# Where tail steps, table turns and weight rounding stand in a recommendation kernel's hand-written order

## The reference

```python
e = jnp.stack([tbl_0[ids[:, 0]], ..., tbl_25[ids[:, 25]]], axis=1)   # 2048 x 26 x 128
combined = jnp.concatenate([e, dense_x[:, None, :]], axis=1)
interact = jnp.einsum('bfd,bgd->bfg', combined, combined)            # 27 x 27 each sample
z = interact[:, _TRIU_I, _TRIU_J]                                    # 351 pairs
h = jnp.concatenate([z, dense_x], axis=1)
h = jnp.maximum(h @ W_top1 + b_top1, 0.0)                            # 479 -> 512
h = jnp.maximum(h @ W_top2 + b_top2, 0.0)                            # 512 -> 256
y = h @ W_top3                                                       # 256 -> 1
```

## Time and profile before

| | us |
|---|---|
| Median of 3 runs | 474.73 (464.82 to 482.69) |
| The profiled execution | 459.81 |
| Its span in the trace | 458.0 |
| PE busy | 431.6 (94%) |
| ACT busy | 282.5 (62%) |
| POOL busy | 253.6 (55%) |
| DVE busy | 241.7 (53%) |

### The profile page before, as it was taken

One profiled execution on the slowest core, in us unless ns is written; L12 is line 12 of the kernel. 1 busy time (PEld: TensorE's weight loads), 2 busy tenths in 40 slices (PEclk: granted clock), 3 DMA queues, 4 the chain that ended last, 5 costly groups with the idle time before them and its releaser, 6 DMA issues.

```text
span 458.0 us, 8937 instructions
## 1 busy us (share of the span) xinstructions
PE 431.6 (94%) x3418; PEld 406.1 (89%) x3418; DVE 241.7 (53%) x279; ACT 282.5 (62%) x996; POOL 253.6 (55%) x270
## 2 busy tenths in 40 slices
PE   4789999789999999999999999999999999979997
PEld 3679999679998999999999999999999898878896
DVE  3979895731667345581567525682467714411152
ACT  3445746857476665667557674666667575677642
POOL 5556565666566656655665656656565556665000
PEclk9999999899999999999999999999999999999999
DMA  6764333121212211221212211221122211111000
GB/s 180 232 210 130 95 91 102 53 65 57 65 47 64 69 53 47 63 70 43 71 50 60 59 54 47 65 68 42 59 59 63 65 54 46 44 45 46 2 1 0
DMA packets 17706, 31.36 MB, mean 68 GB/s; under 512 B 5594, under 2 KB 8480, under 8 KB 17664
## 3 DMA queue, kind: packets, MB, share of 16 engines
q0 software_dynamic: 8384, 17.19, 13.7%
q1 hardware_dynamic: 8400, 12.81, 8.9%
q10 hardware_dynamic: 880, 0.80, 0.6%
HBM read 30.76 MB, written 0.01 MB: 67 GB/s over the span
## 4 chain that ended last, share of the span: by engine, by line
PE 86%; DMA 5%; ACT 4%; issue 3%; DVE 1%; SPq 1%; ACTq 0%
PE x_ps L589 32%; PE gram_ps L603 25%; PE tail_ps L657 13%; PE x_ps L570 6%; DMA hot_in<-in_tbl 5%; PE tail_ps L636 3%; PE tail_ps L627 3%; ACT gram L386 2%; PE tail_ps L663 1%; DVE onehot L841 1%; ACT xt L363 1%; PE x_ps L692 0%; ACT z L400 0%; PE tail_ps L703 0%; PE x_ps L686 0%
## 5 line engine op out<-in xcount | busy, mean ns | idle before, releaser
L553 POOL DMA_INDIRECT raw<-in_tbl,ids_sb x262 | 252.7, 964 | 168.3 <-issue 91.6
L841 DVE TENSOR_TENSOR onehot<-ids_wide,row_ps 128x1024 fp32r<-128x1024 int16 (+1 forms) x175 | 195.0, 1154 | 84.6 <-PE x_ps L589 67.7
L589 PE MATMUL x_ps<-onehot,hot_hi 128*128 128x256 f32 x616 | 159.5, 294 | 9.1 <-DVE onehot L841 3.8
L386 ACT COPY gram<-gram_ps 32x104 f32<-32x104 f32 x496 | 117.9, 238 | 63.6 <-PE gram_ps L603 50.5
L589 PE MATMUL x_ps<-onehot,hot_lo 128*128 128x256 f32 x616 | 151.7, 282 | 0.0
L603 PE MATMUL gram_ps<-xt 128*128 128x108 f32 x1024 | 129.8, 277 | 2.7 <-ACT xt L791 1.0
L589 PEld LDWEIGHTS x_ps<-onehot,hot_hi 128*128 128x128 f32 x616 | 116.1, 189 | 16.4 <-issue 11.8
L603 PEld LDWEIGHTS gram_ps<-xt 128*128 128x128 f32 x1024 | 121.8, 191 | 5.9 <-ACT gram L386 2.0
L589 PEld LDWEIGHTS x_ps<-onehot,hot_lo 128*128 128x128 f32 x616 | 116.1, 189 | 0.0
L363 ACT COPY xt<-x_ps 128x128 f32<-128x128 f32 (+1 forms) x104 | 47.9, 515 | 41.0 <-PE x_ps L589 35.7
L453 DVE TENSOR_TENSOR h_lo<-h,h_hi 128x256 fp32r<-128x256 f32 x28 | 11.9, 426 | 66.6 <-ACT h L425 53.8
(11 more groups left out here) (74 smaller groups left out, 317.8 us busy)
## 6 DMA issues: line engine op xcount, KB each, us to landing
ids_wide<-in_hot_ids SPq DMA_DIRECT2D x19, 256.0 KB
raw<-in_tbl,ids_sb POOLq DMA_INDIRECT x262
hot_in<-in_tbl SPq DMA_DIRECT2D x14, 256.0 KB, 3.3
hot_in<-in_tbl SPq DMA_DIRECT2D x6, 320.0 KB, 3.8
weights_in_place<-in_w SPq DMA_DIRECT2D x6, 128.0 KB
dense_sb<-in_dense_t ACTq DMA_DIRECT2D x6, 128.0 KB
dense_sb<-in_dense_t SPq DMA_DIRECT2D x2, 128.0 KB
w1d_sb<-in_w SPq DMA_DIRECT2D x2, 128.0 KB
```

Of the source, the lines that this page charges most:

```text
L386: last = copy(gram[rows, :, per_fill * i:per_fill * (i + 1)], src)
L553: nc.gpsimd.indirect_dma_start(out=raw[k][:, f, :], out_offset=None, in_=sources[f], in_offset=bass.IndirectOffsetOnAxis(ap=ids_sb[:, t, f ...
L589: last = nc.tensor.matmul(ps, table[:, chunk_at[j] + c, :], moving[:, c - a, :], start=(c == 0 and table is tables_of[0]), stop=(c == chun ...
L841: nc.vector.tensor_tensor(columns(p), ids_wide[:, it // IDS % IDS_RING, it % IDS, 0:width].unsqueeze(1).to_broadcast([P, n, width]), row_n ...
```

## The change

Five edits in the order and around it:

1. A tail step that was due ahead of a tile's second gram of a pair is put behind that gram, so that grams of a block's first tile come in pairs.
2. `with_turn` spreads a tile's turns evenly over a run of slots, and so between the pieces of an item; copies to `xt` then come in another order than the fills of the banks, and the waits count copies (`copied_no`).
3. The casts of the first layer's weights move from block 0's last grams to three items of block 1's lookup ahead of them, their residues to grams 1, 3 and 5 of block 0's second tile; the second layer's two go to the first two grams of block 1. PE asks for each layer's halves where it needs them.
4. The first layer's weights are padded on the host to blocks of 128 rows, with a semaphore a block; what is computed with them is unchanged.
5. DVE makes an item's first piece ahead of the residue of its table, not behind it.

```diff
-    def with_turn(slots, t, ends):
+    def with_turn(slots, t, first, last):
         n = len(turn_groups[t])
         for g in range(n):
-            slots[ends[-(-(g + 1) * len(ends) // n) - 1]].append(("turn", t, g))
+            slots[first + round(g * (last - first) / (n - 1))].append(("turn", t, g))
...
-            slots += with_turn(slots[-1:] + hot[held:lead], t + 1, [0] + ends if h > 0 else ends[-2:])[1:]
+            n = lead - held
+            slots += with_turn(slots[-1:] + hot[held:lead], t + 1, 0 if h > 0 else n - 7, n - 1)[1:]
...
-            slots += with_turn([[] for _ in range(n_gram + n)], t + 2, [n_gram + g for g in range(n)])
+            slots += with_turn([[] for _ in range(n_gram + 3 * n)], t + 2, n_gram, n_gram + 3 * n - 3)
...
-        for i, steps in before.items():
+        moved = {}
+        for i in sorted(before):
+            second = slots[i] and slots[i][0][0] == "gram" and slots[i][0][1] % 2 == 1
+            moved.setdefault(i + 1 if second else i, []).extend(before[i])
+        for i, steps in moved.items():
             slots[i][:0] = steps
...
-        weights_at_gram = range(gram_block + 1 - len(weight_parts), gram_block + 1)
+        second = [("gram", gram_block + n) for n in range(len(weight_parts) - n_kz)]
+        round_at = [("hot", item_start[nh + 2 + n]) for n in range(n_kz)] + second
+        split_at = [("gram", n_gram + 1 + 2 * n) for n in range(n_kz)] + second
...
-                    sp.dma_start(w1z_at[0:kz[k], k, part], w1[sum(kz[:k]):sum(kz[:k + 1]), part]).then_inc(weights_in, 16)
+                    sp.dma_start(w1z_at[:, k, part], w1[k * P:(k + 1) * P, part]).then_inc(weights_in[k], 16)
...
-                    if what[0] in weights_at_gram:
-                        act.wait_ge(weights_in, n_weights * 16)
-                        hi, _, src = weight_parts[weights_at_gram.index(what[0])]
-                        copy(hi, src).then_inc(weights_rounded, 1)
+                if (kind, *what) in round_at:
+                    n = round_at.index((kind, *what))
+                    act.wait_ge(weights_in[n], 2 * 16)
+                    hi, _, src = weight_parts[n]
+                    copy(hi, src).then_inc(weights_rounded, 1)
...
                 if p == item_start[it]:
-                    if it == first_item[j] and j not in direct:
-                        hot_residue(j)
...
                                         ALU.is_equal).then_inc(piece_ready, 1)
+                if p == item_start[it] and it == first_item[j] and j not in direct:
+                    hot_residue(j)
```

More of the change, by code:

```diff
@@ L189, in build @@
                 lead += 1
-            ends = [end + 1 for end in item_ends(hot[held:lead])[:-1]]
-            slots += with_turn(slots[-1:] + hot[held:lead], t + 1, [0] + ends if h > 0 else ends[-2:])[1:]
-        else:
-            slots += gram_slots(t) + with_turn([[] for _ in turn_groups[t + 1]], t + 1, list(range(len(turn_groups[t + 1]))))
+            n = lead - held
+            slots += with_turn(slots[-1:] + hot[held:lead], t + 1, 0 if h > 0 else n - 7, n - 1)[1:]
+        else:
+            n = len(turn_groups[t + 1])
+            slots += gram_slots(t) + with_turn([[] for _ in range(n)], t + 1, 0, n - 1)
             lead, beside = 0, 0
@@ L226, in build @@
     fill_no = {step: n for n, step in enumerate(fills)}
+    copies = [("hot", s[1]) if s[0] == "held" else ("hot", pieces[s[1]][0]) if s[0] == "hot" else s for s in order
+              if s[0] in ("turn", "held")
+              or (s[0] == "hot" and s[1] + 1 in item_end and pieces[s[1]][0] not in held_items)]
+    copied_no = {step: n + 1 for n, step in enumerate(copies)}
+    assert sorted(map(str, fills)) == sorted(map(str, copies))
     def pieces_made():
@@ L896 @@
     rest = len(halves[0]) - 64
[L897 removed]
+    pair_rows = [halves[0][:rest], halves[1][:P], halves[0][rest:] + halves[1][P:]]
     w1 = np.asarray(inputs["W_top1"])
```

45 lines of the change are left out of this document (25 added, 20 removed).

## The result

The change made the kernel slower: 478.5 us (median of four, 473.85 to 481.56) against 469.77 us of the kernel before, ratio 1.027, 95% interval 1.021 to 1.033. Forecast were 469 us, 458 to 478, and no measurable change. The profiled execution of the change took 479.47 us, that of the kernel before 459.81 us.

The account below looks back on a forecast made before the run. PE was taken as the bound, busy 431.6 of 458.0 us. Terms -4.0 - 0.7 - 1.9 - 2.2 + 3.2 = -5.6 us gave 454.2 from 459.81, scaled by 474.73/459.81 to 469 us, range 458 to 478.

Parts of the forecast that it names:

- Turns between pieces: Lookups: turns between an item's pieces give the ring time to fill, taking half of 3.8 us of PE waits, -1.9 us.
- The warning in the last part: Sign of being wrong: casts between items delay `xt` copies so that PE waits between 57 and 66 us.
- Pairs: First tiles: neighbouring `zt` groups and grams run in a row, 0.5 us in each of four settled blocks, -2.2 us in all.
- The new wait of 0.8 us ahead of part 3: Settled blocks: part 3 waits for part 1's bank, its Relu copies queued behind others; 0.8 us four times, +3.2 us.
- Edits 3 and 5: Column stage: moved casts end waits and the half clock, -4.0 us; start: first piece ahead of the residue, -0.7 us.
- Padding: Weight loads: 128-row blocks use more transfer engines, giving gathers up to 3.0 us; 0 in the sum.
- The gathers set the end: Rival, chance 0.20: PE's savings end in a wait for gathers before the last turns; about 473 us.
- The clock falls again: Rival, chance 0.12: idle PE in the column stage drops the clock again, leaving -3.4 us; scaled 471 us.
- Its remark that the one fall before stood behind the emptiest stretch: Support for the clock rival: the trace's one clock fall in 458 us comes behind its emptiest stretch.
- Slower: Rival, chance 0.06: pairs fill both product banks and PE waits for gram copies in first tiles; +12 us, scaled 487.

Follow-up runs that it names:

- e1: The change with turns put back behind whole items, all else kept: 455.79 us, 1.000 of the kernel before.
- e3: The change with both the turns between pieces and the paired grams undone: 454.98 us, 1.002 of the kernel before.
- k3: The change with a column step that would move behind a gram pair put ahead of it: 464.96 us, 1.016 of the kernel before.
- e2: The change with tail steps put back ahead of each gram group, turns still between pieces: 462.99 us, 1.018 of the kernel before.
- d2: The change with ScalarE made late by three small copies ahead of every second hot item's copy: 471.61 us, 1.034 of the kernel before.
- g1: The change with four x_ps banks instead of three, row numbers read from SBUF: 482.79 us, 1.055 of the kernel before.
- e4: The change with turns back behind whole items and tail steps right behind a pair's second gram: 453.78 us, 0.996 of the kernel before.
- k1: e4 with a column step that would stand inside a pair put ahead of it: 453.07 us, 0.992 of the kernel before; again 453.83 us, 1.001.
- d1: The kernel before with ScalarE made late by three small copies ahead of every second hot item's copy: 459.28 us, 1.012 of the kernel before.
- m3: The kernel before with gathers in bursts of four behind the first 66, nothing else changed: 509.09 us, 1.104 of the kernel before.
- g0: The change, unaltered, run again on chip B: 461.25 us, 1.012 of the kernel before.
- g2: The change with block 0's turns alone at their old places: 458.15 us, 1.009 of the kernel before.
- g3: The change with each settled block's last turn ahead of the held item moved behind the split item: 457.0 us, 1.004 of the kernel before.
- m1: k1 with gathers in bursts of four behind the first 66: 506.74 us, 1.100 of the kernel before; on chip A 443.95 us, 0.978.
- k2: k1 with all gathers in bursts of four in place of three: 452.17 us, 0.998 of the kernel before.

## Why the prediction was wrong

**Edit 2, the failed step.** "Turns between pieces: -1.9, bounds 0 and -3.8". The bound at 0 was wrong: I costed what a turn between pieces fills, and not the bank that a split item keeps. With three banks in a ring, the two fills after an item's first piece decide how soon its bank is wanted again, and here they came inside the item. On chips without late engines the term is +5.5 us with edit 1 there (461.25 against 455.79, on two chips; ratios 1.012 and 1.000, whose intervals touch) and +8.0 us without it (462.99 against 454.98, on one chip; 1.018 and 1.002, apart). In three settled blocks it is +2.7 us, of which 1.9 are waits and 0.8 PE's own longer work. My own row showed the danger: 1.2 us of waits for `xt` copies, which I counted as something to win. The warning in the last part, that casts between items might delay `xt` copies, named the right releaser with the wrong cause.

**Pairs.** The gain is there, but smaller: eight zt records in a row take 0.47 us, as in the earlier trace rows, and PE's busy time in three blocks fell from 156.48 (both back) to 155.69 with edit 1, 0.3 us a block against the 0.5 forecast. The new wait of 0.8 us ahead of part 3 came as worked out: 0.8 at its longest, six times, 3.9 us in all when run again (forecast +3.2 in four); up to 1.4 in the first profile with ScalarE late. Edit 1 as a whole is +0.8 us by the medians (e1 against e3, not resolved) and +1.7 in three blocks, against +1.0 in four. What I missed is the last block: a wait of 2.5 us and a half clock of 10.2 us.

**Edits 3 and 5.** The column stage came 3.5 us shorter (forecast -4.0), with casts at 57.9, 59.8 and 63.2 us. The same stage, counted as the same 187 PE records, took 24.1 to 24.8 us in eight other profiles with the casts moved, but 26.3 us in k3, 27.3 in e2 and d2, 30.8 in e1 and 32.1 in g1, in all of which the clock fell again between 88 and 102 us; so moving the casts shortens the stage but does not keep the clock up. The first gram began at 45.90, in place of 47.4 (forecast 0.6 to 0.9 sooner), which shows nothing: in the other profiles with edit 5 it begins anywhere from 44.89 us (e1) to 48.62 (e4). And block 0's second lookup grew, an item waiting 1.68 us for a copy at 67.9. By the medians the edits are worth nothing (e3 1.002), since the end of e3 is at the gathers: its last turn starts 1.6 us after GpSimd's last gather, as in k1. What they are worth without that limit wasn't measured.

**Padding.** As forecast. The gather behind the weights' first loads waits 1.93 us in place of 4.01; it is 4.16 and 4.02 in d1 and m3, which lack the padding too, and 1.79 to 2.15 in g0, e1, e2 and e3. The last gather is issued at 418.89, not 421.67, but that shows little: with the padding and bursts of three it comes between 418.15 (k1 again) and 429.00 us (e2).

**The rivals.** "The gathers set the end" had 0.20, and it is false for the change (last gather 418.89, last turn 451.39) but true in the profiles of e2, e3, e4 and k1, whose last turn starts 1.6 us after GpSimd is done with the last gather; in e1, g2, g3 and m1 on chip A it comes 5.9 us or more behind it. "The clock falls again" holds, at two other places here and in the column stage of five other profiles. Its remark that the one fall before stood behind the emptiest stretch is not so: PE idled 6.84 us before its first product, and from 6 to 12 us the granted clock was 1.00. "Slower" had 0.06 by way of full gram banks: those waits are 2.4 us in all, so that mechanism is not the one, and the side it stood for was given far too little.

**The size.** On chips without late engines the change is 1.012 of before, on the side of "no measurable change" and yet 2.4% from the 0.988 forecast. The other 1.5% is in part exposure: PE waits for more copies directly, so a late start of ScalarE is paid more often, which d1 and d2 show by their 1.022. The rest is open. I read the earlier trace rows as small waits, and did not ask why ScalarE, free and asked, started late; 18.5 us of that stood in the profile.

## What to carry to other kernels

When a step is put inside another's work, list the buffers the split work holds and count the fills until the same buffer comes round; a ring of three with two fills inside an item leaves no slack at all. Price an order also by who becomes directly waited for, since an engine that starts late costs nothing until it is waited for. And before polishing the bound engine, look how far behind its last transfer it runs: here e3, e4 and k1 ran into it, and m1, which moved it, was the only one clearly faster than the kernel before, and that on one of two chips. An order that wins on one chip can lose on the next, so measure on several before believing a per cent.

## What the runs showed of the hardware

ScalarE and VectorE can start late for no reason that the profile names, by chip: in both first profiles and all four on chip D, and in none of fourteen on three others. In the former ScalarE's such waits are 18 to 58 us and VectorE's 27 to 84; on chips A, B and C 0 to 1.2 us. The mark of the late kind is GpSimd's "issue" row, 92 to 104 us against 53 to 61. Durations did not differ: the mean `xt`, gram and `z` copies agree within 3%. The same program took 506.74 us on one such chip and 443.95 on another, while the kernel before took 457.8 and 456.07 there. Why later bursts of four suffer so much from it (82 to 142 us of such waits on ScalarE and VectorE together) is open.

GpSimd's gather issue was 20% slower (961 to 1155 ns) in the kernel in which VectorE reads a small operand from SBUF and not from PSUM, at no cost to VectorE; the cause is not shown. And half-clock stretches began in or right behind single idle stretches of PE: 3.85 us at 368 and 2.53 at 425 in the change, 4.37 at 417 in k1, 1.95 at 67 in k2. In e2 one began at 90 us behind two waits of 0.93 and 0.98 us, with PE busy 5.02 of the 7.00 us before. The 10.2 us at half clock in the change cost up to 5.1 us, half of them (an estimate).
